# Second attention: value parts moved ahead of the scores, projections moved behind the transposes

## What the reference computes

```python
x = x + _L1_xattn_ref(_layernorm(x), ctx_1024, mask, Wq, Wkv, Wo)
# B, N, M = 4, 512, 1024; 4 heads of 64
q = (x @ Wq).reshape(B, N, H, D).transpose(0, 2, 1, 3)
kv = (context @ Wkv).reshape(B, M, 2, H, D).transpose(2, 0, 3, 1, 4)
attn = einsum('bhnd,bhmd->bhnm', q, k) * SCALE
attn = softmax(where(mask, attn, -inf))
out = einsum('bhnm,bhmd->bhnd', attn, v)
return out.transpose(0, 2, 1, 3).reshape(B, N, C) @ Wo
```

## Time and profile before

| | us |
|---|---|
| median of 3 runs (lowest, highest) | 965.04 (962.65, 968.49) |
| the profiled execution, its own time | 967.79 |
| its span, first to last instruction | 965.9 |
| TensorE busy with matmuls | 894.5 (93%) |
| VectorE / ScalarE / GpSimd busy | 562.0 / 491.3 / 431.3 |
| second attention, about | 384 to 643 of the span |

### The profile page before, as it was taken

How to read it: one execution, slowest core, us unless ns; L and a number is a source line. 1 busy time by engine, 2 the same in 40 slices (tenths; PEclk the granted TensorE clock), 3 DMA queues, 4 the chain that set the end, 5 groups by cost and what they waited for, 6 DMA issues and landing times. The chain is left out here.

```text
span 965.9 us, 19473 instructions
## 1 busy us (share of the span) xinstructions
PE 894.5 (93%) x6189; PEld 766.2 (79%) x6190; DVE 562.0 (58%) x1286; ACT 491.3 (51%) x1044; POOL 431.3 (45%) x374
## 2 busy tenths in 40 slices
PE   6899999868999998779999999988899999999995
PEld 4798989746899996557777777757499999999995
DVE  7875453485566675666566575554764454454452
ACT  5744141354444553475665665545655455455552
POOL 2474341004555573755363462300255555555543
PEclk9999999978999999789999999985999999999998
DMA  9721000275766746611010100019667666676662
GB/s 306 239 95 44 1 1 1 76 248 187 254 228 232 253 157 221 135 44 44 5 63 22 45 1 2 28 52 353 229 184 195 211 200 190 209 203 187 206 198 28
DMA packets 68593, 134.72 MB, mean 139 GB/s; under 512 B 8080, under 2 KB 50704, under 8 KB 63408
## 3 DMA queue, kind: packets, MB, share of 16 engines
q1 hardware_dynamic: 55184, 110.27, 33.4%
q0 software_dynamic: 13344, 23.63, 11.2%
HBM read 109.08 MB, written 21.64 MB: 135 GB/s over the span
## 5 line engine op out<-in xcount | busy, mean ns | idle before, releaser
L1901 PEld LDWEIGHTS d_hps<-d_xg_t,d_xw 128*128 128x128 f32 x1248 | 145.2, 192 | 2.4 <-DVE d_xg_t L2085 1.0
L1799 ACT ACTIVATE x<-d_hps,b 128x128 f32<-128x128 f32 x312 | 89.3, 368 | 113.1 <-PE d_hps L1901 112.9
L1901 PE MATMUL d_hps<-d_xg_t,d_xw 128*128 128x128 f32 x1248 | 145.5, 275 | 0.8 <-DVE d_xg_t L2085 0.8
L883 POOL TENSOR_SCALAR c_prob<-c_prob,c_rinv 128x1024 f32<-128x1024 f32 x64 | 72.4, 1150 | 109.4 <-DVE c_rinv L1338 109.0
L1911 PE MATMUL d_yps<-d_w,d_hid_hi 128*128 x312 | 115.2, 402 | 0.0
L1704 POOL DMA_INDIRECT out_x<-d_y,d_take_slot x39 | 63.1, 1619 | 99.1 <-DVE d_y L2122 89.6
L1331 DVE CUSTOM_DVE_ANT_0 c_prob<-c_sc,c_minf 128x1024 f32<-128x1024 f32 x64 | 75.8, 1221 | 36.6 <-PE c_sc L976 34.4
L2085 DVE TENSOR_SCALAR d_xg_t<-d_take,ln_w,ln_b 128x128 f32<-128x128 f32 x78 | 28.5, 406 | 93.4 <-PE d_take L1890 93.1
L1914 PE MATMUL d_yps<-d_w,d_hid_lo 128*128 x312 | 81.2, 281 | 0.0
L1901 PEld LDWEIGHTS b_hps<-b_xg_t,b_w 128*128 128x128 f32 x624 | 76.7, 195 | 3.6 <-issue 1.9
L989 PE MATMUL c_tp<-const,c_prob 128*128 128x128 f32 x512 | 70.5, 281 | 9.8 <-DVE c_pt L1343 5.2
(11 more groups left out here) (367 smaller groups left out, 2106.6 us busy)
## 6 DMA issues: line engine op xcount, KB each, us to landing
d_xw<-in_w SPq DMA_DIRECT2D x39, 1024.0 KB
b_w<-in_w SPq DMA_DIRECT2D x47, 512.0 KB, 7.6
d_w<-in_w SPq DMA_DIRECT2D x8, 1024.0 KB, 12.3
a_raw<-in_ctx_t SPq DMA_DIRECT2D x8, 512.0 KB, 7.0
a_raw<-in_ctx SPq DMA_DIRECT2D x8, 512.0 KB, 4.6
ybuf<-a_zero SPq DMA_DIRECT2D x2, 2048.0 KB, 12.5
k_stage<-in_ctx_t SPq DMA_DIRECT2D x12, 256.0 KB, 3.0
rows<-b_xn_all SPq DMA_DIRECT2D x1, 2048.0 KB, 12.6
```

The source lines that it names most:

```text
L883: nc.gpsimd.tensor_scalar(prob[w][:], prob[w][:], rinv[:, w:w + 1], 1.0, ALU.mult, ALU.mult).then_inc(s["prob_ready"], 1)
L1799: op = nc.scalar.activation(hid[q][:, h * FH + c, :], src[:, c, :], ACT.Gelu_apprx_tanh, bias=b1[:, ds(e, 1), h * FH + c])
L1901: mm = nc.tensor.matmul(hps[j % 2][h][:, c * P:(c + 1) * P], w1[j % WL][:, k, at:at + P], xg_t[j % 2][:, k, :], start=(k == 0), stop=(k == ...
```

## The change

TensorE's list is put in another order; no instruction is added or dropped. Each unit now has one value part, and it stands directly ahead of the next unit's scores. Where a unit has two k projections or two `turn_x`, the second stands behind both groups of transposes, no longer between them. The v projections move by half a unit, so that units 2 and 3 have two each and, like the two output projections of unit 4, one is still between the groups. The lists of ACT and DVE get the copies in the matching order. A pair's first value part now waits until the pair before has been copied out (it waited for the one before that), and every value part waits for the half of v that it reads. In the first batch, ACT's wait for a transfer (`sum_d3`) stands behind the normalisation of x, no longer ahead of it.

```diff
@@ values
-                if part == 0 and b * 4 + m >= 2:
-                    pe.wait_ge(s["att_ready"], b * 4 + m - 1)
+                pe.wait_ge(s["v_in"], b * 4 + 2 * part + 2)
+                if part == 0 and b * 4 + m:
+                    pe.wait_ge(s["att_ready"], b * 4 + m)
...
@@ tensor
+                if before:
+                    values(b - 1, 2, 0)
...
                 scores(b, 0)
                 if before:
                     k_proj(1, 0, xb[:])
                     turn(b - 1, 7, 0)
-                    values(b - 1, 2, 1)
+                    turn(b - 1, 7, 1)
                     pe.wait_ge(s["k_lo"], b * 4 + 3)
                     k_proj(1, 1, xb[:])
-                    turn(b - 1, 7, 1)
-
+
+                if before:
+                    values(b - 1, 2, 1)
                 scores(b, 1)
...
                 turn(b, 0, 0)
+                turn(b, 0, 1)
+
                 if before:
                     values(b - 1, 3, 0)
-                turn(b, 0, 1)
-                if before:
-                    values(b - 1, 3, 1)
-
                 scores(b, 2)
...
+                if before:
+                    values(b - 1, 3, 1)
+                scores(b, 3)
                 if before:
                     pe.wait_ge(s["v_in"], b * 4 + 2)
                     v_proj(2, xb[:])
-
-                scores(b, 3)
+                turn(b, 2, 0)
                 if before:
                     pe.wait_ge(s["v_in"], b * 4 + 3)
                     v_proj(3, xb[:])
-                turn(b, 2, 0)
+                turn(b, 2, 1)
+
+                values(b, 0, 0)
+                scores(b, 4)
                 pe.wait_ge(s["v_in"], b * 4 + 4)
-                values(b, 0, 0)
-                turn(b, 2, 1)
-
-                scores(b, 4)
...
                     project(b - 1, 0, xb)
                 turn(b, 3, 0)
-                values(b, 0, 1)
                 if before:
                     pe.wait_ge(s["x_ready"], b * 2 - 1)
                     project(b - 1, 1, xb)
                 turn(b, 3, 1)
+                values(b, 0, 1)
                 scores(b, 5)
...
                     turn_x(0, xb)
                 turn(b, 4, 0)
-                values(b, 1, 0)
+                turn(b, 4, 1)
                 if more:
                     pe.wait_ge(s["xn_lo"], b * KD + KD + 1)
                     turn_x(1, xb)
-                turn(b, 4, 1)
-
+
+                values(b, 1, 0)
                 scores(b, 6)
...
                     q_proj(0, xb[:])
+                else:
+                    values(b, 2, 0)
                 turn(b, 6, 0)
-                values(b, 2, 0)
                 turn(b, 6, 1)
 
+            values(B - 1, 2, 1)
             turn(B - 1, 7, 0)
-            values(B - 1, 2, 1)
-            turn(B - 1, 7, 1)
             pe.wait_ge(s["att_ready"], B * 4 - 1)
             pe.wait_ge(s["x_ready"], B * 2 - 2)
             project(B - 1, 0, xb)
+            turn(B - 1, 7, 1)
             values(B - 1, 3, 0)
@@ scalar
                 if before:
+                    keep_first(b - 1, 7, 1)
+                    k_high(b, 1, 1, xb[:])
+
+                if before:
                     keep_heads(b - 1, 2)
-                    k_high(b, 1, 1, xb[:])
-                    keep_first(b - 1, 7, 1)
-
                 q_high(b, 1, xb)
...
                 keep_and_exp(b, 4)
-                if b == 0:
-                    act.wait_ge(s["sum_d3"], 16)
-                keep_heads(b, 0)
                 keep_first(b, 3, 1)
                 if more:
                     for t in range(1 if b else 0, TB):
                         x_norm(b + 1, t)
 
+                if b == 0:
+                    act.wait_ge(s["sum_d3"], 16)
+                keep_heads(b, 0)
...
@@ vector
                 keep_and_inverse(b, 5)
+                keep_second(b, 4, 1)
                 if more:
                     x_low(b + 1, 1, xb)
-                keep_second(b, 4, 1)
```

More of the change, by code:

```diff
@@ L1034, in tensor @@
                 before, more = b > 0, b < B - 1
-                if not before:
+                if before:
+                    values(b - 1, 2, 0)
+                else:
                     pe.wait_ge(s["k_lo"], 4)
@@ L1112, in tensor @@
                 turn(b, 5, 0)
-                values(b, 1, 1)
+                turn(b, 5, 1)
                 if more:
@@ L1117, in tensor @@
                     k_proj(0, 1, xb[:])
-                turn(b, 5, 1)
+                values(b, 1, 1)
                 scores(b, 7)
@@ L1228, in scalar @@
                 keep_first(b, 0, 1)
-                if before:
-                    keep_heads(b - 1, 3)
                 if before:
@@ L1240, in scalar @@
                 if before:
+                    keep_heads(b - 1, 3)
                     keep_v(b, 2, xb[:])
+                keep_first(b, 2, 0)
+                exponentials(b, 3, 0)
+                if before:
                     keep_v(b, 3, xb[:])
-                keep_and_exp(b, 3)
+                exponentials(b, 3, 1)
                 keep_first(b, 2, 1)
@@ L1265, in scalar @@
                 keep_and_exp(b, 5)
+                keep_first(b, 4, 1)
                 if more:
                     x_high(b + 1, 1, xb)
-                keep_first(b, 4, 1)
                 if more:
@@ L1275, in scalar @@
                 keep_and_exp(b, 6)
-                keep_heads(b, 1)
+                keep_first(b, 5, 1)
                 if more:
                     k_high(b + 1, 0, 1, xb[:])
-                keep_first(b, 5, 1)
+                keep_heads(b, 1)
                 if more:
@@ L1284, in scalar @@
                 keep_first(b, 6, 1)
+            keep_heads(B - 1, 2)
             keep_first(B - 1, 7, 0)
-            keep_heads(B - 1, 2)
             keep_first(B - 1, 7, 1)
@@ L1398, in vector @@
                 if before:
+                    keep_second(b - 1, 7, 1)
                     k_low(b, 1, 1, xb[:])
-                    keep_second(b - 1, 7, 1)
                 if b == 0:
@@ L1448, in vector @@
                 keep_and_inverse(b, 6)
+                keep_second(b, 5, 1)
                 if more:
                     k_low(b + 1, 0, 1, xb[:])
-                keep_second(b, 5, 1)
                 both_maxima(b, 7)
```

## The result

The changed kernel takes 991.28 us in the median of 6 runs (986.27 to 999.5), the kernel before 964.68 (960.47 to 968.49): a ratio of 1.0286, 95% interval 1.0231 to 1.0342. It is slower by 26.6 us; the prediction was 988.8, within 977 to 998.

The account below looks back on a forecast made before the run. TensorE's back-to-back list was taken to bound the attention from the middle of batch 0. Added waits less saved tilings, 5.8 + 6.0 + 12.0 = 23.8 us, took the median from 965.04 to 988.8 us, range 977 to 998.

Parts of the forecast that it names:

- What bounds the layer: From the middle of batch 0, TensorE's back-to-back list sets the time; the change can only shorten it or add waits.
- The saved tilings: TensorE's list: fewer changes of the array's tiling, 0.10 us each, save 1.4 us a batch if nothing waits.
- The wait for DVE's copy: Second group of transposes waits for DVE's copy behind both maxima and low part: 1.14 us, 2.2 in unit 5.
- E + 3.93: Earliest start of the second group's second half, in us after the scores end (E), with a low part.
- The sum: Whole attention: batch 0 +5.8, batch 1 +6.0, batch 2 and seven units of batch 3 +12.0; in all +23.8 us.
- the end: Last scores to last projection in batch 3: 16.1 us before and after, so no change within 1 us.
- The value part behind ACT's wait: Batch 0, unit 4: a value part formerly inside TensorE's wait for ACT now follows it, costing 2.1 us.
- The clock: Rival: clock falls in five new gaps, unit 5 and batch 3's units 5 and 6; 10 us more, 999; chance 0.12.
- The no-wait case: Rival: nothing in TensorE's list waits, only saved tilings count; 5.1 us less, 960; chance 0.04.
- the half-hidden case: Rival: waits half hidden as maxima and copies run ahead; about 12 us, 977; chance 0.05.
- such a wait for xb in unit 4 alone: Unit 4: the second output projection waits 0.6 us for DVE's addition, which supplies xb.

Follow-up runs that it names:

- covered: The changed kernel with a value part or projection between the two groups in every unit, DVE's and ACT's copies reordered to match; 959.57 us, ratio 0.9941.
- copy_and_low_between: The changed kernel with DVE's copy and low part both between the two maxima in units 0, 1, 5, 6, 7; 973.9 us, ratio 1.011.
- copy_late: The changed kernel with DVE's copy moved behind the unit's two inverse sums in units 0, 1, 5, 6, 7; 1041.91 us, ratio 1.0804.
- copy_between: The changed kernel with DVE's copy alone moved between the two maxima in units 0, 1, 5, 6, 7; 986.51 us, ratio 1.0198.

## Why the prediction was right

**What bounds the layer.** Right: with TensorE back to back in batches 1 to 3, a pure change of its order could show only as a shorter list or as waits, and the waits came.

**The saved tilings.** Right in sign; the size can be seen only roughly. Taking what was lost (1.14 in units 0, 1, 6 and 7, 2.14 in unit 5, 0.64 in unit 4) from the 69.48 us of batch 1 leaves 62.1, which is 1.1 less than 63.26, where 1.4 was forecast. Unit 7 has the same instructions before and in covered, with one change of tiling fewer: 6.96 and 6.76 us. The Trainium skill ("TensorEngine Tiling (Array Packing)", Key Properties) has the rule that a change of tiling mode drains TensorE. The rows agree that a change costs something, 0.10 us in the earlier trace rows and 0.20 in unit 7. What is saved stood against 7.3 us of waits a batch.

**The wait for DVE's copy.** Right in place, engine and length: E + 3.93 predicted and measured in units with a k projection, 1.14 and 2.14 us lost (1.14 and 2.2 predicted), 0.64 in unit 4 (0.6). That DVE's order makes it, and not the mere neighbourhood of the groups, was argued from the earlier trace rows; copy_and_low_between and copy_late show it, each altering DVE's list alone, by -18 and +50 us beside the changed kernel on the same chip.

**The sum.** Predicted +23.8; the attention measured +26.4 in its first profile. By part: batch 1 +6.2 (6.0); batch 2 and seven units of batch 3, 129.49 - 115.51 = +14.0 (12.0); batch 0 up to unit 6, 51.64 - 47.42 = +4.2, and its units 6 and 7 +2.0 (together 5.8); the end 16.05 instead of 16.12. Of the 2.6 us that are off, 1.6 are the half clock behind one wait; the rest is 0.07 in each of units 1 and 7 and 0.4 in batch 0. That batch 0 came out so near is partly luck. In the two profiles of the changed kernel it took 68.99 and 70.61 us, and its terms come out otherwise. The value part behind ACT's wait takes 3.45 at half clock, against which unit 5, partly at half clock before (8.58), now runs at the full clock (8.43): together 3.3 more, where 2.1 and 1.7 were put. The stretch up to the end of ACT's wait, put at nothing, is 0.9 longer.

**The rivals.** The clock was given 0.12 as a case of all five long waits or none, and 10 us. It is neither: a single wait is or isn't followed by half clock, for 1.4 to 1.6 us and not 2. That is the term that was mis-sized. It goes the way in which both medians, 991.3 and 991.9, miss 988.8; that it is the whole of that difference is not shown. The Trainium skill's page "TensorE: Matmul & The Clock Gate" (A second HAM failure mode: psum-queue depth-cycling) tells of small idle times between groups of matmuls and a clock that goes up and down. I had held that to be unsupported by the rows of before; these profiles agree with it behind some of the waits of about 2 us, and copy_late with its longer ones most. The no-wait case would have needed what covered has, another order on DVE and ACT; the half-hidden case did not occur.

**Not foreseen.** That the low part frees xb behind the same two maxima and can hold TensorE in the same way; the prediction counted such a wait for xb in unit 4 alone. It did no harm in the changed kernel, where the second projection comes late enough, and cost me the expectation of copy_between.

## What to carry to other kernels

When two users of the same PSUM bank are brought side by side, read in the evacuating engine's list, in order, what stands ahead of the evacuation; if that work waits for the busy engine's latest result, it sets the gap, as the two maxima did here. What stood between the two users was their cover: replace it by something that waits for neither evacuation, or move the evacuation ahead in its engine's list first, and follow everything behind it. The 0.1 to 0.2 us saved with a change of tiling here are worth having only where no wait of 1 us takes their place.

## What the runs showed of the hardware that was not expected

The granted clock fell to its half level (1.2 GHz) behind waits of about 2 us in a stretch otherwise full, but only behind some of them, in one execution of the same program behind one, in another behind three: a value part then took 2.94 to 3.58 us instead of 1.95. The granted clock also differs from profile to profile in the stage behind the attention, which no kernel here alters. In the 20 us that begin 10 us after the start of the last projection, the kernel before ran at half clock throughout, the changed kernel for about half of them (us, TensorE busy, granted clock; before, then after):

```profile
651.75:661.75 10.00, 10.00 (x48) 0.50 1.10 355
661.75:671.75 10.00, 9.35 (x45) 0.50 1.09 345
```

```profile
678.46:688.46 10.00, 9.71 (x80) 0.92 1.09 354
688.46:698.46 10.00, 5.28 (x14) 0.50 1.10 348
```

From the last projection to the end of the span that made 965.9 - 641.75 = 324.2 and 986.8 - 668.46 = 318.3 us. A difference of a few us between two single executions of this kernel is therefore no evidence, and neither is the spread of a few runs: covered, with no long waits from batch 1 on, spreads over 12.8 us. Unit lengths at full clock, which repeat to 0.05 us, are.
